# Seven eighths of the first quarter of the spectral weights loaded among images 2 to 15

## The reference, cut to what matters

```
x_ft = rfft2(x)
out_ft[:, :, :16,  :16] = einsum('bixy,ioxy->boxy', x_ft[:, :, :16,  :16], w1)     # w1 = w1_r + 1j w1_i
out_ft[:, :, -16:, :16] = einsum('bixy,ioxy->boxy', x_ft[:, :, -16:, :16], w2)     # w2 = w2_r + 1j w2_i
x1 = irfft2(out_ft);   x2 = einsum('bchw,oc->bohw', x, conv_w) + conv_b
y  = kan_linear(kan_linear(x1 + x2, k1...), k2...);   result = x + gelu(y)
```

## Time and profile before

| | |
|---|---|
| median of 3 runs | 3,696.25 us (3,695.16 to 3,698.87) |
| the profiled execution, its own time | 3,700.55 us |
| its span | 3,698.7 us |
| mean granted clock of TensorE | 0.992 |
| TensorE busy | 3,629.4 us, 98% of the span |
| VectorE busy | 94% |
| ScalarE busy | 91% |
| GpSimd busy | 3% |
| DMA queue of SyncE and its packets (q1) | 265.50 MB, 25.3% of 16 engines' span |

### The profile page before, as it was taken

The page is one execution under the profiler, slowest core; times in us unless marked ns, Lnnn a source line. Parts: engine busy times, 40 slices in busy tenths (PEclk is TensorE's granted clock), DMA queues, the critical chain, the costliest instruction groups (busy, mean ns, idle before and its releaser), DMA issues.

```text
span 3698.7 us, 98607 instructions
## 1 busy us (share of the span) xinstructions
PE 3629.4 (98%) x36932; PEld 1565.2 (42%) x36932; DVE 3480.8 (94%) x3548; ACT 3374.5 (91%) x3510; POOL 116.3 (3%) x140
## 2 busy tenths in 40 slices
PE   8987999999999999999999999999999999999998
PEld 4555657654333333333333333333333333333333
DVE  8875999999999999999999999999999999999997
ACT  4433999999999999999999999999999999999997
POOL 0000000000000000000000000000000000000000
PEclk9998999999999999999999999999999999999999
DMA  9998243432322323223232232322323222232231
GB/s 320 328 214 200 61 120 89 118 93 60 76 69 65 77 58 76 68 66 77 58 76 67 67 74 60 77 66 68 73 61 77 64 70 71 63 77 64 70 73 50
DMA packets 269760, 338.45 MB, mean 92 GB/s; under 512 B 83272, under 2 KB 198824, under 8 KB 267624
## 3 DMA queue, kind: packets, MB, share of 16 engines
q1 hardware_dynamic: 248392, 265.50, 25.3%
q0 software_dynamic: 18720, 67.49, 10.1%
q10 hardware_dynamic: 2560, 4.20, 0.4%
HBM read 248.50 MB, written 88.61 MB: 91 GB/s over the span
## 4 chain that ended last, share of the span: by engine, by line
PE 90%; SPq 1%; issue 1%; DMA 1%; ACTq 0%; ACT 0%; DVE 0%; DVEq 0%
PE l_ps L1241 84%; PE y_banks L1218 3%; PE y_banks L1227 2%; SPq L160 1%; PE y_banks L1260 1%; PE y_banks L1202 1%; PE y_banks L1189 0%; PE y_banks L1241 0%; DMA big<-in_spec_w_i_dram 0%; ACTq L729 0%; ACT mixed L726 0%; DMA rows_scratch<-rows 0%; PE l_ps L1260 0%; DMA modes_scratch<-mixed 0%; PE mix_ps L705 0%
## 5 line engine op out<-in xcount | busy, mean ns | idle before, releaser
L1121 ACT ACTIVATE offset<-size 128x1024 f32<-128x1024 f32 x1280 | 1241.0, 1045 | 8.1
L1047 DVE SCALAR_TENSOR_TENSOR cube0r<-below,offset 128x1024 f32<-128x1024 f32 x256 | 312.6, 1221 | 113.2 <-ACT offset L1121 103.2
L1047 DVE SCALAR_TENSOR_TENSOR cube2r<-below,offset 128x1024 f32<-128x1024 f32 x256 | 311.5, 1217 | 0.6 <-PE l_ps L1241 0.6
L1047 DVE SCALAR_TENSOR_TENSOR cube0l<-above,offset 128x1024 f32<-128x1024 f32 x256 | 311.7, 1217 | 0.0
L1047 DVE SCALAR_TENSOR_TENSOR cube1r<-below,offset 128x1024 f32<-128x1024 f32 x256 | 311.6, 1217 | 0.0
L1047 DVE SCALAR_TENSOR_TENSOR cube1l<-above,offset 128x1024 f32<-128x1024 f32 x256 | 311.6, 1217 | 0.0
L1047 DVE SCALAR_TENSOR_TENSOR cube3r<-below,offset 128x1024 f32<-128x1024 f32 x256 | 311.5, 1217 | 0.0
L1047 DVE SCALAR_TENSOR_TENSOR cube2l<-above,offset 128x1024 f32<-128x1024 f32 x256 | 311.5, 1217 | 0.0
L1047 DVE SCALAR_TENSOR_TENSOR cube3l<-above,offset 128x1024 f32<-128x1024 f32 x256 | 311.5, 1217 | 0.0
L1047 DVE SCALAR_TENSOR_TENSOR cube4l<-above,offset 128x1024 f32<-128x1024 f32 x256 | 311.4, 1217 | 0.0
L1047 DVE SCALAR_TENSOR_TENSOR cube4r<-below,offset 128x1024 f32<-128x1024 f32 x256 | 311.4, 1216 | 0.0
(11 more groups left out here) (169 smaller groups left out, 5963.3 us busy)
## 6 DMA issues: line engine op xcount, KB each, us to landing
big<-in_x_dram SPq DMA_DIRECT2D x128, 512.0 KB, 8.3
x_ring<-in_x_dram SPq DMA_DIRECT2D x256, 256.0 KB, 4.6
out_dram<-act_out SPq DMA_DIRECT2D x128, 512.0 KB, 2.6
act_out<-in_x_dram POOLq DMA_DIRECT2D x127, 512.0 KB, 7.0
rows_t<-rows_scratch SPq DMA_DIRECT2D x512, 32.0 KB
rows_scratch<-rows SPq DMA_DIRECT2D x14, 1024.0 KB, 6.8
pair_t<-pair_scratch SPq DMA_DIRECT2D x128, 65.0 KB, 1.9
big<-in_spec_w_r_dram SPq DMA_DIRECT2D x16, 512.0 KB, 11.6
```

Of the source, the lines that this page charges most:

```text
L1047: nc.vector.scalar_tensor_tensor(out=cube[q][side][:], in0=distance[own][:], scalar=EDGE - KNOTS[q], in1=offset[own][q][:], op0=ALU.min, o ...
L1121: nc.scalar.activation(offset[own][q][:], size[own][:], ACT.Square, bias=-KNOTS[q]).then_inc(offset_ready[layer], 1)
```

## The change

The first seven eighths of w1_r (output channels 0 to 55) are no longer loaded behind the image loop. They are loaded in it: behind the eight pieces of image b, for b from 2 to 15, SyncE loads output channels 4 (b - 2) to 4 (b - 2) + 3, 256 KB, in two transfers of 128 KB (one for each half of the x modes). They go to the same place in slot 2 as before. The wait for `weights_turned` moves with them into the loop. The last eighth (channels 56 to 63) is loaded behind the loop by `load_mix_weights`, whose last chunk may now be shorter than 16 channels. The mix's wait for w1_r now counts 30 transfers (14 x 2 and 2) instead of 8.

```diff
+O_IMAGE = 4
+O_AMONG = O_IMAGE * (B - 2)
+
+
+def load_mix_weights_among(sp, t, dst, image):
+
+    for half in range(2):
+        x0 = SH * half
+        sp.dma_start(dst[half * C:(half + 1) * C, bass.ds((image - 2) * O_IMAGE, O_IMAGE), :, :],
+                     t["w1_r"][:, bass.ds((image - 2) * O_IMAGE, O_IMAGE), x0:x0 + SH, :]).then_inc(t["mix_loaded"][0][0], 16)
...
     for o0 in range(o_first, o_end, MIX_O):
+        o1 = min(o0 + MIX_O, o_end)
         for half in range(2):
             x0 = SH * (half if g == 0 else 1 - half)
-            sp.dma_start(dst[half * C:(half + 1) * C, o0:o0 + MIX_O, :, :],
-                         src[:, o0:o0 + MIX_O, x0:x0 + SH, :]).then_inc(t["mix_loaded"][g][part], 16)
+            sp.dma_start(dst[half * C:(half + 1) * C, o0:o1, :, :],
+                         src[:, o0:o1, x0:x0 + SH, :]).then_inc(t["mix_loaded"][g][part], 16)
...
             with sp.Fori(1, B // 2) as b2:
                 for par in range(2):
                     next_image(b2, par)
+                    sp.wait_ge(weights_turned, len(TURNS))
+                    load_mix_weights_among(sp, t, weights[:, 2], 2 * b2 + par)
 
             sp.wait_ge(consts_loaded, 160)
-            sp.wait_ge(weights_turned, len(TURNS))
-
-            load_mix_weights(sp, t, weights[:, 2], 0, 0, 0, C)
+
+            load_mix_weights(sp, t, weights[:, 2], 0, 0, O_AMONG, C)
             load_mix_weights(sp, t, weights[:, 3], 0, 1, 0, C // 2)
...
-                    pe.wait_ge(t["mix_loaded"][g][part], 32 * (C // MIX_O))
+                    pe.wait_ge(t["mix_loaded"][g][part], 32 * (C // MIX_O if g + part else B - 1))
```

## The result

The changed kernel's median is 3,706.61 us (3,699.09 to 3,713.32, 7 runs) against 3,695.6 us for the kernel before (3,693.02 to 3,699.38, 7 runs). The ratio is 1.0029, 95% interval 1.0020 to 1.0039. Timed again later, it was 3,706.96 us (12 runs) against 3,697.72 us (24 runs), ratio 1.0022, interval 1.0014 to 1.0031. (The ratios are estimated from all executions of both kernels, so they can differ from the quotient of the medians by some hundredths of a per cent.) The time lies above my range (3,692.5 to 3,704), and the way it went is rival A, to which I gave 0.08.

The account below looks back on a forecast made before the run. The forward part was taken as bound by TensorE, with 20 weight pieces behind the boundary setting the mix's end. 0 removed from the chain and 0 added gave 3,696.5 us, range 3,692.5 to 3,704.

Parts of the forecast that it names:

- rival A: Forward part: loads become its bound if X is over 1.8 us; +7.8 us at 2.4; chance 0.08 of over 0.2% slower.
- What bounds the kernel: Forward part bound by TensorE; queue empty five microseconds before the 248.7 us block boundary; 20 weight pieces behind it set the end.
- Removed, gain 0: Seven w1_r issues at 205 us removed: 19.4 us of queue time, none on the chain, so gain 0.
- X: Cost of 256 KB of weights in an image's full load queue: taken as 1.6 us, between 1.39 and 3.0.
- The part per transfer (0.14 us): In the load queue, the cost of a transfer whatever its size, fitted from image and weight pieces: 0.14 us.
- The estimate of 10 us: Forward part: 2.6 us for two 128 KB transfers by the Trainium skill, end 10 us later; set aside.
- The bound of 3.0 us: Load queue: upper bound of X, if all of an image piece's time is fixed cost, 2 x 1.51 = 3.0 us.
- the threshold of 1.8 us: Forward part: the X at which TensorE's spare time before image 15's last piece reaches nothing, 23.5 / 13 = 1.8 us.
- 13 (X - 1.8): Forward part: how late images arrive if X is over 1.8 us; +7.8 us at 2.4, +15.6 at 3.0.
- The cushion: Forward part: time between an image's last piece landing and TensorE needing it; 3.8 us at image 3 before, 2.6 forecast at 15.
- SyncE's vanished waits for TensorE: Image loop: SyncE's 27.5 us of waits for TensorE between images would be nearly gone, listed as a sign of being right.

Follow-up runs that it names:

- the four profiles: The changed kernel, unaltered, profiled four times: the profiled executions took 3,699.1, 3,704.1, 3,703.1 and 3,698.8 us.
- the fifth: Profile of the changed kernel with its third stage left out and one image copied to the result; its unprofiled median is 357.63 us.
- The cut kernels: Kernel before and changed kernel, each with its third stage left out and one image copied to the result: 350.85 us against 357.63 us.

## Why the prediction was wrong

**What bounds the kernel: right.** The forward part was bound by TensorE, with an empty queue ahead of the boundary, and 20 pieces behind it set the end.

**Removed, gain 0: right.** The kernel with the weights left out shows it (1.0002, 0.9992 to 1.0011).

**X: wrong, and this is the step that failed.** "I take 1.6, nearest to the rows of the weight pieces themselves." It measured 2.20 us (2.01 to 2.18 over eight images in the four profiles). I priced a weight transfer by the rate of weights among weights (2.78 us for 512 KB) and of images among images, and added. Both rates are right, and the sum is not: 14.25 us for an image with its weights, where the separate rates give 12.05 + 1.39. The packets show which part was missing. The 1.39 us "by packets alone" is near what the weights' own packets took of each DMA engine (1.40 us). That they also make the image pieces' packets longer, by 1.36 us per image, had no term in the sum: I put it at nothing. The part per transfer (0.14 us) that I added in its place has no run that shows it. The rows had a sign of it. A weight piece and an image piece have the same 512 KB, and the first takes 1.84 times as long; I read all of that as the price of 512-byte runs. It is mostly the destination: each weight transfer writes 64 partitions, each image piece 128, and a packet of the same 512 bytes took 54.0 ns into 64 partitions and 30.6 into 128. The Trainium skill (SBUF — State Buffer, "Door 1: The DMA port swizzle") says that 64 partitions from 0 or from 64 reach only 8 of 16 ports, for about half of the bandwidth. The trace agrees, 186 against 348 GB/s, of which the shorter runs are the smaller part, by the packets just named. That a transfer of that kind also slows the full-width transfers beside it is what the runs add: 232 GB/s while they mix, image packets of 76.5 ns in place of 50.9. It is not that half of the DMA engines stood idle, as their share was 1.17. That it is the ports, and not something else about half of the partitions, was not tried.

**The estimate of 10 us came near, and its reason did not hold.** Against itself the prediction set an X of 2.6 us and 10 us in the end, worked out from the Trainium skill (DMA: Bandwidth & Descriptors, "Measured"), and put it aside because the x pieces overlap. By number it was nearer than mine. But it priced a transfer by its size alone. Here two transfers of the same 128 KB cost 0.90 us into 128 partitions, and one of 256 KB, for which the same line gives an estimate of 2.0 us against 2.6 for two of 128, was not cheaper.

**The bound of 3.0 us held, and the threshold of 1.8 us too, in direction.** By my own formula 13 (X - 1.8) is 5.2 us at X = 2.20, and in that profile the boundary moved by 7.4. (Over four profiles it moved by 5.0 to 7.9 us, 9.2 in the fifth.) Part of what is over lies in a thing that the formula lacks: image 2's last piece, ahead of any weights, was issued at 39.16 us and landed 9.8 us later, at 49.0 us and not at 47.9 as before. The weights behind it, issued from 40.72 us, were already under way. The later images' last pieces landed 9.4 to 10.2 us after their issue, those read before 8.3 to 8.7. The cushion is 1.1 us smaller from the start, so the first lost time is at image 3 (a step of 13.87 us) and not in images 9 to 15, where I had told the reader to look.

**A sign that could not tell.** I listed SyncE's vanished waits for TensorE under "right". They vanished, but they would under rival A too: a full queue waits for nothing else.

**Rival A: right in mechanism, and underrated.** I wrote that the cushion was thin and gave it 0.08. A margin of 0.2 us on a price that no row had (1.6 against 1.8) did not bear 0.88. That the profiled execution took 3,699.1 us, where I had 3,700.6, is luck: its first two stages took 4.3 us more than before and its third 5.7 less.

**How much of the 9 to 11 us is explained.** The cut kernels differ by 6.8 us; that lies inside the second interval (5 to 11 us) and a little under the first (7.4 to 14). The profiles' 3.9 to 5.7 us at the inverse transform are lower, the fifth's boundary higher. With no cushion left, X itself differs from execution to execution (2.01 to 2.42 us), and the delay with it. A remainder of 2 to 4 us is not told apart from chance here, and stays open.

## What to carry to other kernels

A transfer's price in a full queue is not its own rate alone: measure it among the transfers that it will run beside, and ask what it does to them. Transfers that fill half of the partitions cost 2.4 times as much here as the same bytes over all of them. Before moving loads forward, look whether the queue is empty ahead of the point that they wait for: if it is, nothing can be gained by it. What paid here was to lift what kept later loads behind that point (7 us).

## What the runs showed that was not expected

One 256 KB transfer into 64 partitions per image cost 2.61 us, and two of 128 KB into the two halves 2.0 to 2.4 us. A stage that does not differ between kernels took 3,358.8 to 3,365.5 us; in the profile of before, an estimated 4.6 us of that lie in one place that the changed kernel's profile lacks: TensorE idles 2.91 us ahead of 777.71 us, and from 778.3 us on 3.4 us are granted at the clock's lower level, 1.2 GHz, where they do half of the work. So for a change worth a few microseconds in a stage, the stage's own marks say more than the total of one execution.
